# A 16-layer forward pass on one core: v of the 64-dim-head attention projected into PV's PSUM bank before the turnings, and the scan's u times D summed on TensorE

## The reference

```python
def step(h, inp):                       # over the tokens, state (b, 256, 16)
    dA_t, dBu_t, c_t = inp
    h = dA_t * h + dBu_t
    y = jnp.einsum('bdn,bn->bd', h, c_t)
    return (h, y)
y = _selective_scan(x_b, delta, a, b, c)
y = y + x_b * D_param
y = y * jax.nn.silu(res)
return y @ out_proj_w.T + out_proj_b
```

```python
q = (jnp.einsum('bnd,ed->bne', y, Wq) + bq).reshape(b_s, n, H, D_K).transpose(0, 2, 1, 3)
k = ...; v = ...                        # the same with Wk, bk and Wv, bv
att = jax.nn.softmax(jnp.einsum('bhqd,bhkd->bhqk', q, k) * scale, axis=-1)
out = jnp.einsum('bhqk,bhkd->bhqd', att, v)
out = jnp.einsum('bne,de->bnd', out.transpose(0, 2, 1, 3).reshape(b_s, n, H * D_V), Wo) + bo
```

## Time and profile before

| | |
|---|---|
| median of 3 runs | 3105.68 us (3104.74 to 3111.06) |
| the profiled execution's own time | 3102.63 us |
| its span, first to last instruction | 3100.8 us |
| TensorE matmuls busy | 2725.2 us, 88% of the span |
| VectorE / ScalarE / GpSimd busy | 62% / 45% / 35% |
| mean granted TensorE clock | 0.947 |
| the scan stage's second half | from 78 to 331 us |
| the 64-dim-head attention stage | from 1737 to 2096 us |

### The profile page before, as it was taken

The page is one execution under the profiler, slowest core; times in us unless marked ns, Lnnn a source line. Parts: engine busy times, 40 slices in busy tenths (PEclk is TensorE's granted clock), DMA queues, the critical chain, the costliest instruction groups (busy, mean ns, idle before and its releaser), DMA issues. The chain is left out here.

```text
span 3100.8 us, 62274 instructions
## 1 busy us (share of the span) xinstructions
PE 2725.2 (88%) x24165; PEld 1790.4 (58%) x24165; DVE 1915.6 (62%) x4333; ACT 1395.4 (45%) x2898; POOL 1098.9 (35%) x1448
## 2 busy tenths in 40 slices
PE   7999699978799968897888799997999979889997
PEld 2343367756467755565555576664666657556664
DVE  7889554556455566634674566665677736556764
ACT  5656144434244435422453345443555524345553
POOL 4878444224344223312112333330222236312223
PEclk9899799999799988879999999998999999999999
DMA  2000200011000001110101000002222201112221
GB/s 81 1 1 1 79 18 19 7 25 29 25 18 20 7 1 46 51 47 18 32 22 31 16 1 1 1 1 67 62 83 72 72 19 30 56 45 76 71 83 47
DMA packets 62498, 107.09 MB, mean 35 GB/s; under 512 B 8138, under 2 KB 47062, under 8 KB 61440
## 3 DMA queue, kind: packets, MB, share of 16 engines
q1 hardware_dynamic: 56832, 94.63, 10.2%
q0 software_dynamic: 5376, 8.47, 1.0%
HBM read 79.66 MB, written 23.86 MB: 33 GB/s over the span
## 5 line engine op out<-in xcount | busy, mean ns | idle before, releaser
L569 ACT ACTIVATE s_sT<-s_R 128x1024 f32<-128x1024 f32 (+2 forms) x448 | 415.6, 947 | 157.5 <-PE s_R L500 157.3
L604 DVE TENSOR_REDUCE s_negm<-s_R 128x4 f32<-128x1024 f32 x320 | 376.6, 1219 | 87.8 <-PE s_R L471 85.5
L471 PE MATMUL s_R<-s_qk 32*128 32x256 f32 (+2 forms) x3584 | 241.8, 382 | 94.3 <-ACT s_sT L569 67.0
L500 PE MATMUL s_R<-s_qA,s_qk 32*128 32x256 f32 (+2 forms) x3584 | 241.3, 383 | 20.5 <-DVE s_negm L604 12.6
L622 DVE TENSOR_TENSOR s_qA<-s_qk,s_OB 128x256 f32<-128x256 f32 x224 | 94.2, 421 | 265.7 <-PE s_OB L543 259.0
L471 PEld LDWEIGHTS s_R<-s_qk 32*128 32x128 f32 x3584 | 159.2, 185 | 144.8 <-issue 122.4
L520 PE MATMUL s_OB<-s_sT,s_v 128*32 128x256 f32 (+2 forms) x3584 | 225.7, 370 | 10.2 <-ACT s_sT L569 6.4
L500 PEld LDWEIGHTS s_R<-s_qA,s_qk 32*128 32x128 f32 x3584 | 163.2, 185 | 105.5 <-issue 102.4
L576 ACT ACTIVATE s_oc<-s_OB 128x256 f32<-128x256 f32 x224 | 85.8, 383 | 272.1 <-PE s_OB L520 268.0
L1519 POOL TENSOR_TENSOR s_pr<-s_pr,s_rinv 128x1024 f32<-128x1024 f32 x64 | 121.1, 1893 | 220.0 <-DVE s_rinv L1629 220.0
L1601 ACT ACTIVATE s_pr<-s_S,s_negmax 128x256 f32<-128x256 f32 x256 | 118.5, 470 | 135.5 <-DVE s_negmax L1632 135.5
(11 more groups left out here) (611 smaller groups left out, 6206.3 us busy)
## 6 DMA issues: line engine op xcount, KB each, us to landing
s_wB<-enc_b SPq DMA_DIRECT2D x32, 962.5 KB, 4.7
s_scratch<-s_pk SPq DMA_DIRECT2D x58, 256.0 KB, 2.0
s_qk<-s_scratch SPq DMA_DIRECT2D x232, 64.0 KB
s_wA<-enc_a SPq DMA_DIRECT2D x32, 193.0 KB, 3.9
big<-moe SPq DMA_DIRECT2D x2, 2347.0 KB, 10.8
all_W<-weights SPq DMA_DIRECT2D x2, 2199.5 KB, 12.8
big<-routed SPq DMA_DIRECT2D x2, 2084.0 KB
s_returned<-s_back SPq DMA_DIRECT2D x2, 1024.0 KB
```

What stands on the lines that cost most here:

```text
L471: last = pe.matmul(S[h][:, t * T:t * T + hi - lo], b.qk[rows, r % 2, 0, c, t * P:(t + 1) * P], b.qk[rows, r % 2, 1, c, lo:hi], start=(t == ...
L500: last = pe.matmul(b.R[:, a.turned_at(u, h // 2), :][:, h % 2, a.at(kt)], b.qk[rows, r % 2, 1, c, kt * P:(kt + 1) * P], b.qA[rows, u % 2, ...
L569: act.activation(b.sT[:, u % (a.lag + 1), 2 * p:2 * p + 2, 0:a.width], b.R[:, a.turned_at(u, p), 0:a.width], ACT.Exp).then_inc(s.expd, 1)
L604: ins = dve.tensor_reduce(b.negm[:, u % 2, :, at].rearrange("p t h -> p h t"), S.rearrange("p h (t k) -> p h t k", t=TT), AX_X, ALU.max, n ...
```

## The change

In the attention stage v's two matmuls move ahead of the turnings and into the free right half of the bank O (columns 256 to 511) with two semaphores of their own, `v_mm` and `v_cp`. Since ScalarE's reads and TensorE's writes of one bank are kept apart, v waits until the PV before has been read out (`oT_cp`), and PV waits until this step's v has been read out (`v_cp`). ScalarE's copy of v moves ahead of all four exponentials. In X only q, k and the Wo product remain.

In the scan stage ScalarE makes, once at the start, two diagonal matrices `skip` (identity times D, L2822 of the changed file). At each chunk's first state TensorE multiplies u by them into Y (start=True) and adds the 16 states to it. `finish` is one multiplication, gate by Y straight from PSUM. The matmuls of a new chunk wait for `gated` of the chunk before, as before, but that semaphore now rises when the gate's multiplication has ended.

```diff
     def fronts(u):
-        return [("qk", u + FRONT), ("v", u + FRONT)] if u + FRONT < U else []
+        return [("qk", u + FRONT)] if u + FRONT < U else []
...
                         last.then_inc(x_mm, 1)
+                        if u > PV:
+                            pe.wait_ge(oT_cp, u - PV)
+                        if w:
+                            pe.wait_ge(v_cp, w)
+                        for t in range(TT):
+                            tile = b * T + t * P
+                            last = pe.matmul(O[:, T + t * P:T + (t + 1) * P], g.hT[:, tile:tile + P],
+                                             wv[:, c * P:(c + 1) * P], start=True, stop=True, skip_group_check=True)
+                        last.then_inc(v_mm, 1)
                     j = u - TURN
...
-                    if w < U:
-                        use_bank(("v", w))
-                        for t in range(TT):
-                            tile = b * T + t * P
-                            last = pe.matmul(X[:, t * P:(t + 1) * P], g.hT[:, tile:tile + P],
-                                             wv[:, c * P:(c + 1) * P], start=True, stop=True)
-                        last.then_inc(x_mm, 1)
...
-                        pe.wait_ge(x_used, number[("v", j)] + 1)
+                        pe.wait_ge(v_cp, min(w + 1, U))
                         pe.wait_ge(prT_cp, j + 1)
...
+                    w = u + FRONT
+                    if w < U:
+                        act.wait_ge(v_mm, w + 1)
+                        act.activation(v[:, w % 6, :, :], O[:, T:2 * T].rearrange("p (t n) -> p t n", t=TT), ACT.Copy)\
+                           .then_inc(v_cp, 1)
                     if 0 <= u < U:
                         act.wait_ge(maxed, u + 1)
                         exps(0)
-                    w = u + FRONT
-                    if w < U:
-                        act.wait_ge(x_mm, number[("v", w)] + 1)
-                        act.activation(v[:, w % 6, :, :], X[:, 0:T].rearrange("p (t n) -> p t n", t=TT), ACT.Copy)\
-                           .then_inc(x_used, 1)
-                    if 0 <= u < U:
                         exps(1).then_inc(expd, 1)
```

```diff
+            skip = ss.sb("skip", [P, M, P])
...
                         j = q - 2
                         if j >= 0:
-                            first, last_ = j % N == 0, j % N == N - 1
+                            c = j // N
+                            if j % N == 0:
+                                pe.wait_ge(skip_made, M)
+                                if c:
+                                    pe.wait_ge(gated, c)
+                                for m in range(M):
+                                    pe.matmul(Y[:, m, :], skip[:, m, :], u[:, m, c * C:(c + 1) * C], start=True,
+                                              stop=False, skip_group_check=True)
                             pe.wait_ge(hcs, j + 1)
-                            if first and j:
-                                pe.wait_ge(gated, 2 * (j // N) - 1)
                             for m in range(M):
-                                last = pe.matmul(Y[:, m, :], g.ident[:], hc[:, j % 2, m, :], start=first, stop=last_)
+                                last = pe.matmul(Y[:, m, :], g.ident[:], hc[:, j % 2, m, :], start=False,
+                                                 stop=(j % N == N - 1), skip_group_check=True)
                             last.then_inc(summed, 1)
...
                     copy_b(0)
+                    for m in range(M):
+                        act.activation(skip[:, m, :], g.ident[:], ACT.Copy, scale=g.w("m_d")[:, m:m + 1])\
+                           .then_inc(skip_made, 1)
...
-                        for m in range(M):
-                            ins = dve.scalar_tensor_tensor(out=yv[:, m, :], in0=u[:, m, c * C:(c + 1) * C],
-                                                           scalar=g.w("m_d")[:, m:m + 1], in1=Y[:, m, :],
-                                                           op0=ALU.mult, op1=ALU.add)
-                        ins.then_inc(gated, 1)
-                        dve.wait_ge(gated, 2 * c + 1)
-                        dve.tensor_tensor(yv[:], yv[:], gate[:, :, c * C:(c + 1) * C], ALU.mult).then_inc(gated, 1)
+                        dve.tensor_tensor(yv[:], Y[:], gate[:, :, c * C:(c + 1) * C], ALU.mult).then_inc(gated, 1)
```

More of the change, by code:

```diff
@@ L1503, in wide_attention_stage @@
         X = st.ps("X", [P, 512])
-        (bias, bo_added, x_mm, x_used, scored, maxed, expd, recip, normed, turned, prT_cp, pv, oT_cp) = [
-            st.sem(n) for n in ("bias", "bo_added", "x_mm", "x_used", "scored", "maxed", "expd", "recip", "normed",
-                                "turned", "prT_cp", "pv", "oT_cp")]
+        (bias, bo_added, x_mm, x_used, v_mm, v_cp, scored, maxed, expd, recip, normed, turned, prT_cp, pv, oT_cp) = [
+            st.sem(n) for n in ("bias", "bo_added", "x_mm", "x_used", "v_mm", "v_cp", "scored", "maxed", "expd", "recip",
+                                "normed", "turned", "prT_cp", "pv", "oT_cp")]
         nx = BatchNorms(st, 0, "next")
@@ L2747, in mamba_stage @@
             Y = ss.ps("Y", [P, M, C])
-            (cleared, bb_mm, bb_cp, cb_mm, cb_cp, exps, dbu_low, dbu_high, scans, hcs, summed, gated, out_mm,
-             added) = [ss.sem(n) for n in ("cleared", "bb_mm", "bb_cp", "cb_mm", "cb_cp", "exps", "dbu_low",
+            (cleared, skip_made, bb_mm, bb_cp, cb_mm, cb_cp, exps, dbu_low, dbu_high, scans, hcs, summed, gated, out_mm,
+             added) = [ss.sem(n) for n in ("cleared", "skip_made", "bb_mm", "bb_cp", "cb_mm", "cb_cp", "exps", "dbu_low",
                                            "dbu_high", "scans", "hcs", "summed", "gated", "out_mm", "added")]
@@ L2770, in outputs @@
                     def outputs(c):
-                        pe.wait_ge(gated, 2 * (c + 1))
+                        pe.wait_ge(gated, c + 1)
                         for t in range(4):
```

## The result

The changed kernel takes 3065.97 us (median of 4 runs, 3062.8 to 3066.89) against 3105.21 (4 runs), a ratio of 0.987 with a 95% interval of 0.9855 to 0.9886: 39 us faster, where 28 were forecast, and 1 us below the range. One later execution of the changed kernel took 3893 us at a mean granted clock of 0.635; it is of the slow state and is left out of all means.

What follows compares the result with a forecast made beforehand. TensorE was taken to bound the attention, its v matmuls waiting for k out of X; TensorE, VectorE and GpSimd nearly fill the scan. Terms -25.8, -4 and +1.5 sum to -28.3 us: forecast 3077 us, range 3067 to 3092.

Steps and rivals of the forecast that it cites:

- added wait: Attention: v waits for the last PV's copy out of O, PV for this step's v copy; both forecast to cost nothing.
- all five pieces: Attention step between TensorE starts: scores, q and k, v, turnings, PV; 4.90 us falling to 4.47, over 60 steps 25.8 us.
- The slack of 0.3 us ahead of PV: Attention: v's copy ends 3.16 us after the scores, PV wants to start at 3.45, so it fits.
- The attention's start: First four attention steps, without PV: removing v's waits for k gains 4 us (2 to 6).
- four long waits: v's waits in the four attention steps without PV, 1.40 us in the first, about 5 together; part comes back.
- The chunk ends: Three chunk ends inside the scan: shorter finish against added matmuls, together +0.7 us (-2.7 to +2.7).
- Tail: Scan's end: finish of 1.41 us goes and 1.23 stays, -1.4 us (to -3 if the clock stays up).
- Start: Scan's start: two small ScalarE instructions +0.5, added matmul pair ahead of the first Y +1.7, together +2.2 us.
- Bare loads: Rival, attention: first weight loads of v or the turnings are not hidden under earlier matmuls; 3089 us, chance 0.12.
- PV takes over the wait: Rival, attention: ScalarE reaches v's copy 0.4 us later, PV stalls by v's gain; 3098 to 3106 us, chance 0.06.
- the ring through O: Rival, attention: v, its copy, exponentials and PV's copy wait in a circle; at 5.1 us a step 3118 us, chance 0.03.
- The scan gives more back: Rival, scan: all four added matmul pairs run exposed at 1.2 GHz; 3081 us, chance counted inside the forecast's 0.77.

Runs made afterwards that it cites:

- the two reordered kernels: Attention change alone on the kernel before, with v issued behind the turnings: 3102.2 us; or with ScalarE's copy of v between the exponentials: 3086.9 us.

## Why the prediction was wrong

**The direction and the mechanism were right.** TensorE's wait for k out of X was the bound, its removal gives 0.44 us a step (0.43 forecast), the loads are hidden, and neither added wait is felt. From the scores of unit 2 on the stage is 26.4 us shorter, against 25.8. That this is so near is in part luck: PV starts with step 3, so 59 steps and not 60 hold all five pieces, and step 3 gave 0.75 us (5.21 to 4.46) while step 2 gave nothing (4.20 to 4.28). The slack of 0.3 us ahead of PV, the term I leaned on most, is 0.39, and taking it away costs what was said.

**The sum was too small by 11 us, 0.6 of it in the steps and the rest in four places.**

1. *The attention's start, 4 us forecast (2 to 6), 7.0 measured.* I let part of the four long waits come back through the reciprocal ahead of the next maximum. In the profile only 0.77 us comes back, and the denser start brought the second q and k to 2.4 GHz, which I had not counted at all. Outside my bounds, 3.0 of the 11. Over all profiles the new start is 11.9 to 12.5 us and the old 18.4 to 19.3, 6.4 us apart in the means, so 0.6 of the 7.0 is of this pair of profiles.
2. *The chunk ends, +0.7 forecast, -2.3 measured (-0.77 each).* The arithmetic at full clock was right (-0.9 against -0.77). The failed step is "at two of the three ends the clock stood at 1.2 GHz": I carried the clock of the old trace over to a new order with more work for TensorE behind its pause. In 12 ends of four profiles with the new order the clock cost something at 3; why it stays up there, and fell at all three ends without the added pair, is open. That is 3.0 of the 11.
3. *The scan's other terms.* Tail -1.4 forecast, -2.6 measured: the output matmuls started at 2.4 GHz, the end of the range I had named. Start +2.2, measured +0.6 for the two small instructions and +1.1 for the first Y. The three steps behind the outputs, 44.4 us in all before, took 0.9 less. Together 2.6.
4. *Untouched stages, 0 forecast, -2.3 in this pair of profiles.* I put them at nothing because no code changes there. Ahead of and between the touched stages single executions differ as much with no change of code (1404.1 and 1411.2 us between them in two profiles of the kernel before). Behind the attention the profiles with the shorter step have 4 us less in the mean of 13, and I have no cause for them.

**The rivals.** Bare loads: refuted by the load rows. PV takes over the wait, and the ring through O: neither seen; the two reordered kernels show that the first is real with the copy 0.7 us later (0.34 of the 0.44 us a step are lost), and that it takes all of the step's gain when v stands behind the turnings. The scan gives more back: wrong, the scan stage became 4 us shorter in the profile.

**The range** was the failure of judgement. With a term or two at their ends the sum reached 3070, and the range left 3 us below that, though single runs of this kernel scatter by 5 us and an omitted term of clock was to be expected on the fast side as much as on the slow.

## What to carry to other kernels

Price a removed wait joint by joint, from rows of the same pair of matmul kinds: it gave the step to 0.02 us. Where a wait moves to another engine's copy, look at where that copy stands in its own engine's order; here the position among four exponentials was worth 22 of 33 us. Added work on a nearly full engine belongs into that engine's pauses: the same two matmuls cost the scan step 1.7 us at a chunk's start (4.92 against 3.22) and nothing at its end.

## What the runs showed that I had not expected

- Leaving out four pairs of matmuls did not help: the scan stage was 254.0 instead of 254.5 us and the median of the runs 7 us higher (3103.5 against 3096.6), with TensorE at 1.2 GHz where it had mostly stood at 2.4: Y took 3.39, 3.57 and 3.52 us at the three chunk ends instead of 1.88, behind pauses of about the same length (1.85 and 1.89). Neither the fall of the clock nor the higher median is explained.
- The gate's multiplication of 1024 elements takes 1.20 us with one operand in PSUM beside a busy GpSimd. With both in SBUF it took 2.24 in the middle of the stage and 1.23 at its end, where GpSimd was idle. At the first chunk's end before:

```profile
142.88 2.35 POOL L2849 TENSOR_TENSOR all_hT<-s0s_hs,s0s_cb 128x1024 f32<-128x1024 f32 x1
144.08 2.24 DVE L2891 TENSOR_TENSOR s0s_yv<-s0s_yv,s_gate 128x1024 f32<-128x1024 f32 x1
145.19 1.79 POOL L2837 TENSOR_TENSOR s0s_dBu<-s_du,s0s_bb 128x288 f32<-128x288 f32 x1
```

  The Trainium skill names this in "GPSIMD Engine Reference" (Specifications): VectorE instructions with two SBUF inputs contend with GpSimd for the SBUF interfaces. The trace agrees: VectorE's multiplication is about 1 us too long where GpSimd's first product still ran for 1.15 us, and GpSimd's second product, 0.79 us away from the chunk ends, is 1 us too long beside VectorE's.
- The attention's steps at full clock repeat to 0.01 us between executions (303.20 or 303.21 in seven profiles), while stages in which the clock falls now and then differ by several us (1402 to 1411 for those between scan and attention).
